# Gate loops in rounds of three steps: PSUM on every third step, products in place in a ring of eight buffers

## The reference, cut to what matters

```python
def _gate(h, q, Wg, bg, Wq, bq):
    B, L, F = q.shape                 # 8 graphs, 64 queries, 768 features
    N = h.shape[0] // B               # 32 nodes in a graph
    h3 = h.reshape(B, N, F)
    hg = jnp.einsum('bnf,gf->bng', h3, Wg[:, :F])
    qg = jnp.einsum('blf,gf->blg', q, Wg[:, F:]) + bg
    attn = jax.nn.sigmoid(hg[:, :, None, :] + qg[:, None, :, :])
    qi = jnp.einsum('bnlf,blf->bnf', attn, q)
    ...
```

## Time and profile before

| | |
|---|---|
| median of 3 runs | 1108.97 us (1108.43 to 1109.07) |
| span of the profiled execution, first to last instruction | 1107.1 us |
| what the runs have more than that span | 1.9 us |
| gate loop 0, first triple of sums to the end | 179.17 to about 284.6 us |
| gate loop 1 | 405.9 to about 511.7 us |

### The profile page before, as it was taken

The page is one execution under the profiler, slowest core; times in us unless marked ns, Lnnn a source line. Parts: engine busy times, 40 slices in busy tenths (PEclk is TensorE's granted clock), DMA queues, the critical chain, the costliest instruction groups (busy, mean ns, idle before and its releaser), DMA issues.

```text
span 1107.1 us, 17712 instructions
## 1 busy us (share of the span) xinstructions
PE 1058.3 (96%) x7444; PEld 882.3 (80%) x7444; DVE 765.8 (69%) x1089; ACT 572.9 (52%) x606; POOL 260.8 (24%) x160
## 2 busy tenths in 40 slices
PE   6999999999999999999999989899999999999987
PEld 5889986545799974546689689758999999999984
DVE  8794755888653158886454665656888888888862
ACT  0432226888433268885233544325666666666630
POOL 3524706898200048984000000000000000000000
PEclk9999999999999999999999999999999999999999
DMA  8143256222044372220444004408777777777720
GB/s 291 12 149 110 86 184 188 58 58 59 17 155 172 124 228 67 69 58 1 157 172 172 29 1 172 167 1 299 257 243 251 245 255 249 256 256 248 255 98 28
DMA packets 82291, 163.18 MB, mean 147 GB/s; under 512 B 4044, under 2 KB 60136, under 8 KB 81918
## 3 DMA queue, kind: packets, MB, share of 16 engines
q1 hardware_dynamic: 80736, 151.86, 41.1%
q0 software_dynamic: 1472, 10.15, 3.3%
HBM read 158.35 MB, written 0.80 MB: 144 GB/s over the span
## 4 chain that ended last, share of the span: by engine, by line
PE 80%; DVE 13%; issue 4%; ACT 2%; POOL 1%; DVEq 0%; POOLq 0%; ACTq 0%
PE PS L1085 19%; PE PS L766 7%; PE PS L937 7%; PE PS L782 5%; PE PS L688 5%; PE PS L577 4%; PE PS L1068 4%; PE PS L1099 4%; PE PS L507 4%; PE PS L664 4%; PE PS L520 3%; PE PS L589 3%; PE PS L1002 2%; PE PS L824 1%; DVE arena L1663 1%
## 5 line engine op out<-in xcount | busy, mean ns | idle before, releaser
L1912 DVE TENSOR_TENSOR Wlo<-W,Whi 128x2304 fp32r<-128x2304 f32 x68 | 173.7, 2556 | 43.5 <-ACT Whi L1419 43.4
L1419 ACT CAST Whi<-W 128x2304 fp32r<-128x2304 f32 x68 | 144.5, 2126 | 0.0
L1085 PE MATMUL PS<-Whi,Mhi 128*128 128x384 f32 x408 | 137.9, 338 | 0.0
L1085 PE MATMUL PS<-Wlo,Mhi 128*128 128x384 f32 x408 | 136.5, 334 | 0.0
L1085 PE MATMUL PS<-Whi,Mlo 128*128 128x384 f32 x408 | 136.4, 334 | 0.0
L474 POOL TENSOR_TENSOR PRDP<-arena 128x1024 f32<-128x1024 f32 x48 | 114.7, 2389 | 32.1 <-issue 19.6
L766 PE MATMUL PS<-QH,SEL 128*128 128x512 f32 x384 | 115.7, 422 | 5.4 <-ACT xT L1256 1.4
L1277 ACT ACTIVATE arena<-PS 128x1024 f32<-128x1024 f32 x96 | 98.4, 1025 | 23.8 <-PE PS L766 23.8
L766 PEld LDWEIGHTS PS<-QH,SEL 128*128 128x128 f32 x384 | 64.8, 188 | 55.3 <-DVE PRD L1663 21.0
L1277 ACT ACTIVATE PS<-PS 128x1024 f32<-128x1024 f32 x96 | 98.0, 1021 | 2.6 <-PE PS L766 2.6
L1085 PEld LDWEIGHTS PS<-Whi,Mlo 128*128 128x128 f32 x408 | 76.8, 188 | 0.0
(11 more groups left out here) (295 smaller groups left out, 2497.8 us busy)
## 6 DMA issues: line engine op xcount, KB each, us to landing
W<-in_L_rel SPq DMA_DIRECT2D x68, 1152.0 KB, 5.7
W<-in_W_rel SPq DMA_DIRECT2D x6, 2304.0 KB, 9.4
W<-in_W SPq DMA_DIRECT2D x6, 2304.0 KB, 9.1
arena<-in_qU SPq DMA_DIRECT2D x96, 128.0 KB, 2.6
W<-in_WqT SPq DMA_DIRECT2D x4, 2304.0 KB, 9.8
W<-in_W_root SPq DMA_DIRECT2D x2, 2304.0 KB, 13.7
W<-in_WgT SPq DMA_DIRECT2D x2, 2304.0 KB, 9.5
QH<-QH POOLq DMA_DIRECT2D x2, 1536.0 KB, 9.9
```

Of the source, the lines that this page charges most:

```text
L1085: mm = pe.matmul(PS[:, 4 + s % 2, 0:HALF], MS[a][mb][:, k, j * P:(j + 1) * P], WS[b][w % 3][:, k, :], start=n == 0, stop=n == 17)
L1419: nc.scalar.copy(WS[0][w % 3][:], W[(FIRST34 + r) % 2][:, :, q * HALF:(q + 1) * HALF]).then_inc(w_hi, 1)
L1912: V.tensor_tensor(WS[1][w % 3][:], W[(FIRST34 + r) % 2][:, :, q * HALF:(q + 1) * HALF], WS[0][w % 3][:].bitcast(F32), ALU.subtract).then_i ...
```

## The change

The steps are sorted anew, the sigmoid that stays in SBUF goes into a ring of eight buffers (RING[c % 8]), and the product overwrites it there, on DVE and on POOL alike. Where the sigmoid is in PSUM, the product is written to RING[c % 8]. SIGS, SIGP, PRD and PRDP go. Of 96 steps POOL keeps 24 (2, 5 and 10 of each 12), and DVE 72. The steps with the sigmoid in PSUM are now every third one, 32 in place of 48, so that of DVE's products 32 read PSUM and 40 read two operands in SBUF, where it was 48 and 24. PE does the sums of three steps, and then the column sums of three older steps. ACT, and DVE for a product out of PSUM, wait for the column sums of step c - 8 before they write a ring buffer; the waits of ACT for products and of POOL and DVE for product buffers go.

```diff
+POOL_STEPS = (2, 5, 10)
 def on_pool(n):
-    return n % 4 == 2
+    return n % 12 in POOL_STEPS
 def in_psum(n):
-    return n % 2 == 1
+    return n % 3 == 0
...
-                for c in range(2, STEPS, 4):
+                for c in filter(on_pool, range(STEPS)):
                     u, h, k = c // UB, c // QUADS % 2, by_pool(c)
-                    if c % QUADS == 2:
-                        pool.wait_ge(qd_in[h], 64 * (g * UNITS + u + 1))
+                    pool.wait_ge(qd_in[h], 64 * (g * UNITS + u + 1))
                     pool.wait_ge(attn_done, g * STEPS + c + 1)
-                    if k >= 2:
-                        pool.wait_ge(red_done, g * STEPS + c - 7)
-                    nc.gpsimd.tensor_tensor(PRDP[k % 2], SIGP, QD[h], ALU.mult).then_inc(pool_prod, 1)
+                    nc.gpsimd.tensor_tensor(RING[c % 8], RING[c % 8], QD[h], ALU.mult).then_inc(pool_prod, 1)
...
-                for c in range(2, STEPS + 4, 2):
-                    if c < STEPS:
-                        sums(c)
-                        sums(c + 1)
-                    if c >= 4:
-                        reduce(c - 4)
-                        reduce(c - 3)
...
+                for c in range(0, STEPS, 3):
+                    for i in range(c, c + 3):
+                        if i >= 2:
+                            sums(i)
+                    for i in range(max(c - 4, 0), c - 1):
+                        reduce(i)
...
-                    elif on_pool(c):
-                        out = SIGP
-                        if c >= 4:
-                            act.wait_ge(pool_prod, by_pool(g * STEPS + c))
                     else:
-                        out = SIGS
-                        if c >= 4:
-                            act.wait_ge(prod_done, by_dve(g * STEPS + c - 3))
+                        out = RING[c % 8]
+                        if c >= 8:
+                            act.wait_ge(red_done, g * STEPS + c - 7)
...
-                    if k >= 4:
-                        dve.wait_ge(red_done, g * STEPS + (k - 4) // 3 * 4 + (0, 1, 3)[(k - 4) % 3] + 1)
-                    sig = PS[:, at_banks(c):at_banks(c) + 2, :].rearrange("p b n -> p (b n)") if in_psum(c) else SIGS
-                    V.tensor_tensor(PRD[k % 4], sig, QD[h], ALU.mult).then_inc(prod_done, 1)
-                    if u and c % UB == 9:
+                    if in_psum(c):
+                        sig = PS[:, at_banks(c):at_banks(c) + 2, :].rearrange("p b n -> p (b n)")
+                        if c >= 8:
+                            dve.wait_ge(red_done, g * STEPS + c - 7)
+                    else:
+                        sig = RING[c % 8]
+                    V.tensor_tensor(RING[c % 8], sig, QD[h], ALU.mult).then_inc(prod_done, 1)
+                    if u and c % UB == 8:
                         copy_sum(u - 1)
```

More of the change, by code:

```diff
@@ L71, in sums_bank, with by_pool @@
     return 0 if n == 1 else 4
+def by_pool(n):
+    return n // 12 * len(POOL_STEPS) + sum(k < n % 12 for k in POOL_STEPS)
 def by_dve(n):
-    return n - (n + 1) // 4
-def by_pool(n):
-    return (n + 1) // 4
+    return n - by_pool(n)
 R3, R34 = 3, 34
@@ L159, in build @@
         QH = [put(f"QH{h}", [P, UNITS, GATE_B, THIRD], F32R, 24 + 24 * h) for h in range(2)]
-        SIGS, SIGP = (view(arena, 7936 + 1024 * i, 1024) for i in range(2))
-        PRD = [view(arena, 9984 + 1024 * i, 1024) for i in range(2)] + [put(f"PRD{i}", [P, 1024], F32, 92 + 4 * i)[:] for i in (2, 3)]
-        PRDP = [put(f"PRDP{i}", [P, 1024], F32, 4 * i)[:] for i in range(2)]
+        RING = [put(f"RING{i}", [P, 1024], F32, at)[:] for i, at in enumerate((84, 100, 104, 0, 72, 76, 80, 4))]
         QD = [view(arena, 12032 + 1024 * i, 1024) for i in range(2)]
@@ L774, in reduce @@
                         pe.wait_ge(pool_prod, by_pool(g * STEPS + c) + 1)
-                        made = PRDP[by_pool(c) % 2]
                     else:
                         pe.wait_ge(prod_done, by_dve(g * STEPS + c) + 1)
-                        made = PRD[by_dve(c) % 4]
+                    made = RING[c % 8]
                     if i == 0 and u >= 2:
@@ L803, in turn_sums @@
                     mm.then_inc(qi_turned, 1)
-                for c in range(2, STEPS + 4, 2):
-                    if c < STEPS:
-                        sums(c)
-                        sums(c + 1)
-                    if c >= 4:
-                        reduce(c - 4)
-                        reduce(c - 3)
[L812 to L815, removed]
+                for c in range(0, STEPS, 3):
[4 more added lines that the diff above has]
+                        reduce(i)
+                reduce(STEPS - 4)
+                reduce(STEPS - 3)
+                pe.wait_ge(qi_copied, UNITS * (g + 1) - 1)
+                turn_sums(0)
+                turn_sums(1)
+                reduce(STEPS - 2)
+                reduce(STEPS - 1)
                 weights(m0 + 6)
@@ L1655, in _ @@
                         continue
-                    k = by_dve(c)
                     if i == 0:
```

## The result

| | before | after |
|---|---|---|
| median | 1108.85 us (1108.43 to 1109.07, 4 runs) | 1130.32 us (1129.99 to 1132.74, 4 runs) |
| span of the profiled execution | 1107.1 us | 1128.3 us |
| gate loop 0, first triple of sums to L824 / L823 | 179.17 to 284.61: 105.4 us | 178.09 to 294.58: 116.5 us |
| gate loop 1, likewise | 405.94 to 511.66: 105.7 us | 414.93 to 531.18: 116.3 us |

The ratio is 1.0202 (95% interval 1.019 to 1.0215). The change makes the kernel 21.5 us slower, where 21.6 was forecast. The two loops alone took 21.6 us more (11.1 + 10.5) and the span 21.2. The stretch before loop 0 is 1.1 us shorter, that between the loops 1.0 shorter, and that behind loop 1 1.7 us longer, which nearly cancels.

The account below looks back on a forecast made before the run. PE set the pace, POOL and DVE having little air; now SBUF access shared by DVE and POOL would stretch rounds from 13.07 to 14.4 us. Sixteen rounds add 21.3 to 1107.1, plus 1.9: 1130.5 us; 8-in-10 range 1116 to 1152.

Parts of the forecast that it names:

- The one thing that both need, and its holds: Gate loops: two-SBUF-operand DVE products and POOL instructions exclude each other; holds 1.09 us (DVE), 2.26 (POOL product), 0.43 (piece).
- The hand-overs: Gate loops: a waiting DVE or POOL instruction starts about 0.13 us before the other engine's instruction ends.
- The round laid out by hand: Gate loops, 12 steps, first asked first served: closes at 14.2 us, or 14.55 with the subtraction.
- The sum: Gate loops: 14.4 - 13.07 = 1.33 us a round, 16 rounds cost 21 us; 1130.5 us in all.
- the clock: PE's idle times may lower its granted clock: +0 to +8 us on top, no case of its own.
- the copy: Gate loops: a copy of 0.42 us behind step 8, expected in one round of four.
- What costs nothing: ACT's sigmoids, ACT's and DVE's new waits, query loads: no cost; loop start and end 0 +- 1 us.
- Rival 1, DVE keeps the access: Gate loops: DVE's next product goes ahead of a waiting POOL; round 15.6 us, +40, 1149 us; chance 0.28.
- Rival 2, well packed: Gate loops: DVE's and POOL's requests fall into each other's gaps; round 13.5 to 14.0, 1116 to 1124 us; chance 0.12.
- Rival 3, faster: Gate loops: stretched times have another cause than DVE's second SBUF operand; round 12.7 us, 1103 us; chance 0.08 for a gain.
- the banks' chain: Gate loops: sums, sigmoid in PSUM, DVE product, back to PE: 3.09 us for three steps, 12.36 for twelve at best.
- The rule weighed: Skill's issue-order rule: the piece that asked first runs before DVE's 8, keeping 14.4 us; one earlier row disagrees, giving 15.6.

Follow-up runs that it names:

- experiment 1: The changed kernel with POOL's products cut to 8 of their 1024 columns, POOL's pieces kept: 1103.29 us.
- experiment 2: The changed kernel with DVE's 80 two-operand SBUF products replaced by reductions of the same 1024 elements through one operand, POOL's work kept: 1103.69 us.
- experiment 6: The changed kernel with each of DVE's two-operand SBUF products issued as two halves of 512 columns with no wait between: 1168.83 us.
- experiment 5: The changed kernel with POOL's 22 splitting pieces moved behind each gate loop: 1168.67 us, of which some 24 are the pieces.
- experiment 8: The changed kernel with POOL only at steps 2 and 5 of 12 and PSUM on 3, 4, 6 and 7: 1118.28 us, ratio 1.0092 to before.

## Why the prediction was right, point by point

- *The one thing that both need, and its holds.* Right, and now shown rather than inferred: experiments 1 and 2. The hand-overs read in the changed kernel fit the 0.13 us read before.
- *The round laid out by hand.* It said 14.2 to 14.55 us; the round read above is 14.28. With t = 0 at 224.70, the start of the sums of step 6, DVE's 7 ends at 5.0 (said 5.25), 8 at 6.7 (6.6 to 6.9), 9 starts at 6.6 (6.5 to 6.85), the next sums at 7.9 (7.8 to 8.1), POOL's 10 ends at 8.9 (8.8), DVE's 11 at 10.0 (9.9). PE's long wait is 1.71 us (about 1.6). Only the longest two-operand product is off: 2.74 us, where up to 2.3 was said.
- *The sum.* Its total is right by luck; two terms of it are off by some 5 us each and cancel. It counted 16 rounds of 1.33 us over before, 21.3. In the trace only the 14 rounds from the sums of step 9 to those of step 93 of each loop (7 x 2) lost time; what is left at the two ends of a loop differs from before by 0.2 and 0.0 us. Without the clock these rounds take 13.7 us (a triple of 4.1 in place of 4.8), 14.3, 14.4 or 14.6, in the mean 14.2 and not 14.4: 14 x 1.15 = 16.1 us. The rest, 5.3 us, came from what the forecast named and set at nothing in its sum: the clock. Four times in the two loops the granted clock fell to the lower of its two levels for 3.4 us, and before, both loops stood at 1.00. The first time it stood so (columns as in the earlier trace rows):

```profile
247.57:250.98 3.41, 3.41 (x18) 1.84 (x20) 3.18 (x3) 2.83 (x3) 1.99 (x2) 0.50 0.14 40
```

  It came behind PE's wait of 2.03 us; the sums that follow take 2.63 us in place of 1.66, and a triple 4.6 in place of 3.3. The round of 15.90 us (0.89 in its row) is this one, against 14.4 for the same steps in gate loop 1. That is about 1.3 us each. The net price is somewhat less, as the round behind each of the two falls in mid-loop took 13.7. Two slips have no weight: 1107.1 + 21.3 + 1.9 is 1130.3 and not 1130.5, and the copy stands behind step 8 of a round once in 96 steps (step 56), not in one round of four.
- *What costs nothing.* Right for ACT's and DVE's waits for column sums: none of them appears among the waits of the loops, where ACT waits for sums only; nor does a wait for the queries. The stretches outside the loops were to be equal within 1 us; the last is 1.7 us longer.
- *Rival 1, DVE keeps the access.* Fell, in the changed kernel itself (the subtraction between 7 and 8) and in experiment 6. Rounds near its sum (15.6 us) did turn up, with another cause, in experiment 5. Why the one POOL instruction of the earlier trace rows took 10.26 us stays open, and it is no accident of one trace: the same instruction has 10.26 us in the changed kernel's and 10.27 in that of experiment 1.
- *Rival 2, well packed.* Did not occur in this kernel. Something like it shows in experiment 8, where five rounds of seven took 12.8 to 12.9 us with POOL and DVE both at work.
- *Rival 3, faster.* Its sum, 1103 us, is what experiments 1 and 2 measured once the exclusion was taken away: the banks' chain of 3.09 us shows as 3.09 and 3.10 in every kernel here with threes wherever no triple was held up, and the three successive products in a round of 12.71 and 12.67 us, typical of those two runs.
- *The rule weighed.* The Trainium skill's "Issue order, not op shape, decides who blocks" (SBUF — State Buffer, "Who interferes with whom") held in every meeting of the gate loops that was read, experiment 6 included; it does not fit the one of the earlier trace rows.

## What to carry to other kernels

Before moving an operand from PSUM to SBUF to free banks, count DVE's instructions that then read two operands in SBUF while POOL works: here 16 more a loop, at no change in anybody's own work, cost 11 us a loop. Adding up how long each engine holds the shared access gives a floor, not the time. Who asks first matters as much, so lay one period out in order, and expect that an edit that lightens POOL can make it worse (experiment 5) and that cutting instructions in two adds meetings (experiment 6). A total that fits is no proof of its terms: here 16 rounds in place of 14 made up for a clock set at nothing.

## What the runs showed of the hardware that was not expected

- A POOL instruction that waits is let in between two DVE instructions issued back to back with no wait: the second half of 0.68 us took 1.22, and the median of all 80 was 0.88 (experiment 6).
- A DVE reduction of 1024 fp32 elements out of SBUF (one operand) takes 1.21 us beside POOL at work, all 80 within 14 ns, as long as the product of two operands takes alone (1.22).
- Four intervals of 3.4 us at the lower clock, about 1.3 us each, appeared behind idle times of PE of 1.8 to 2.0 us, in loops that had none before. Such idle times are not enough: those at 218.30 (1.83 us) and 484.69 (2.02 us) were followed by none, and the loops of experiment 5, where PE was idle for longer in all but never for more than 1.1 us at once, stood at 1.00 throughout. What decides stays open.
